# Softmax sums turned as one small transpose and spread through DRAM, the 256-key scores in split precision, another order of the query tiles, and the zero fills moved

## The reference, cut to what matters

```python
xn = _layernorm(x, axis=-1)                       # x: 8 batches x 512 tokens x 256
out = x + attention(xn) + moe(xn)                 # both in float32

# attention: 16 heads, latent keys/values of 64, rotary part of 64
norm_q  = rmsnorm(xn @ W_cq, q_scale);  norm_kv = rmsnorm(xn @ W_ckv, kv_scale)
scores  = einsum('bhqd,bhkd->bhqk', query, key) * scale      # 512 x 512 a head
attn    = softmax(where(causal, scores, -1e9), axis=-1)
attn_out = einsum('bhqk,bhkd->bhqd', attn, value) @ W_o

# moe: 32 experts, top 6, plus a shared expert
routed = einsum('tef,efd,te->td', silu(x@wg) * (x@wu), wd, combine)
```

## Time and profile before

| | |
|---|---|
| median of three runs | 1375.63 us |
| the profiled execution | 1372.54 us |
| its span | 1370.8 us |
| TensorE busy | 1268.6 us, 93% |
| VectorE busy | 898.7 us, 66% |
| ScalarE busy | 902.1 us, 66% |
| GpSimd busy | 631.3 us, 46% |
| stages, from the span's start | `project` from 30.2, `heads_first` from about 201, `experts` from 611, `heads_last` from about 960 us |

### The profile page before, as it was taken

The page is one execution under the profiler, slowest core; times in us unless marked ns, Lnnn a source line. Parts: engine busy times, 40 slices in busy tenths (PEclk is TensorE's granted clock), DMA queues, the critical chain, the costliest instruction groups (busy, mean ns, idle before and its releaser), DMA issues. The chain is left out here.

```text
span 1370.8 us, 25128 instructions
## 1 busy us (share of the span) xinstructions
PE 1268.6 (93%) x7640; PEld 999.6 (73%) x7641; DVE 898.7 (66%) x2823; ACT 902.1 (66%) x2462; POOL 631.3 (46%) x550
## 2 busy tenths in 40 slices
PE   4899859999999899979999999998899999999997
PEld 3566547778777678758788888887678777877775
DVE  3578778988888788823333333332787888788783
ACT  1455428777777587735566666665797788788783
POOL 1111108877776677730000000000888878878881
PEclk8899979999999999999999999999899999999999
DMA  9988663323236532239876666664555655655652
GB/s 347 362 288 283 258 234 117 111 98 115 97 110 231 175 105 97 90 110 338 320 247 188 188 181 199 186 186 148 108 84 86 103 107 89 128 86 97 104 70 47
DMA packets 150870, 223.32 MB, mean 163 GB/s; under 512 B 13846, under 2 KB 128214, under 8 KB 149462
## 3 DMA queue, kind: packets, MB, share of 16 engines
q1 hardware_dynamic: 102934, 157.72, 34.4%
q0 software_dynamic: 36864, 53.50, 19.0%
q10 hardware_dynamic: 10944, 10.49, 2.5%
HBM read 105.27 MB, written 116.39 MB: 162 GB/s over the span
## 5 line engine op out<-in xcount | busy, mean ns | idle before, releaser
L1580 POOL DMA_INDIRECT l_sums<-sorted_y,slot_no x192 | 308.1, 1605 | 59.3 <-issue 57.6
L1072 POOL DMA_INDIRECT sorted_x<-f_xn_row,slot_no x192 | 198.2, 1032 | 49.2 <-issue 44.5
L2184 DVE SCALAR_TENSOR_TENSOR act_f<-hidden,rows_in,ps 128x96 f32<-128x96 f32 x224 | 70.4, 314 | 228.5 <-ACT hidden L2147 228.4
L1257 ACT ACTIVATE f_prob<-f_prob,f_negmax 128x256 f32<-128x256 f32 (+3 forms) x256 | 142.7, 558 | 84.1 <-DVE f_negmax L1345 82.0
L2109 PE MATMUL ps<-wgu_sb,xt_e 128*128 x896 | 184.2, 328 | 0.4 <-issue 0.2
L1762 ACT ACTIVATE l_prob<-l_prob,l_negmax 128x256 f32<-128x256 f32 (+3 forms) x256 | 141.6, 554 | 62.1 <-DVE l_negmax L1862 60.7
L1587 POOL TENSOR_TENSOR l_k_lo<-l_kt,l_k_hi 128x512 fp32r<-128x512 f32 x4 | 5.1, 1273 | 368.7 <-ACT l_k_hi L1755 368.7
L1862 DVE CUSTOM_DVE_ANT_0 l_prob<-ps,mask_add 128x256 f32<-128x256 f32 (+3 forms) x256 | 119.9, 486 | 51.4 <-PE ps L66 37.6
L1345 DVE CUSTOM_DVE_ANT_0 f_prob<-ps,mask_add 128x256 f32<-128x256 f32 (+3 forms) x256 | 117.7, 482 | 45.5 <-PE ps L66 40.5
L2109 PEld LDWEIGHTS ps<-wgu_sb,xt_e 128*128 128x128 f32 x896 | 140.0, 190 | 3.2 <-issue 2.6
L2127 PE MATMUL ps<-wd_sb,at 96*128 x448 | 139.1, 392 | 1.1 <-issue 0.5
(11 more groups left out here) (212 smaller groups left out, 3168.9 us busy)
## 6 DMA issues: line engine op xcount, KB each, us to landing
sorted_x<-zeros SPq DMA_DIRECT2D x14, 2304.0 KB, 9.9
rows_in<-sorted_x SPq DMA_DIRECT2D x112, 288.0 KB, 3.2
sorted_y<-rows_out SPq DMA_DIRECT2D x112, 256.0 KB, 2.1
wgu_sb<-in_wgu SPq DMA_DIRECT2D x16, 384.0 KB, 5.7
x_in<-in_x SPq DMA_DIRECT2D x8, 512.0 KB, 10.5
xn_dram<-xn SPq DMA_DIRECT2D x8, 512.0 KB, 3.9
base_dram<-x_in SPq DMA_DIRECT2D x8, 512.0 KB, 2.9
nqt_dram<-nqt_out SPq DMA_DIRECT2D x8, 512.0 KB, 3.9
```

Of the source, the lines that this page charges most:

```text
L1072: pool.indirect_dma_start(sorted_x, bass.IndirectOffsetOnAxis(ap=slot_no[:, t, k:k + 1], axis=0), xn_row[buf][:], None).then_inc(scattered ...
L1257: act.activation(prob[:, i, qt, 0:w], prob[:, i, qt, 0:w], ACT.Exp, bias=negmax[:, i, qt:qt + 1], scale=-1.0, accum_out=rowsum[:, g // 2 % ...
L1580: pool.indirect_dma_start(sums[n % NSUM][:, t, :], None, sorted_y, bass.IndirectOffsetOnAxis(ap=slot_no[:, TT * GROUPS[n] + t, k:k + 1], a ...
```

## The change

1. The sums are turned before the reciprocal is taken: one transpose of `rowsum` (128 x 8) to 8 x 128, at the end of the even step, after `scores(3)`. VectorE takes the reciprocal of 8 partitions x 128 numbers from PSUM, after `maxima(3)` and ahead of `turned`.
2. SyncE stores the 8 x 128 inverses to `norms_dram`, waits for that, and loads them back, repeated over 64 partitions, with two transfers into `norms`. `spread_inverses`, `turn_norms` and `copy_norms` go from GpSimd, ScalarE and TensorE.
3. `FIRST_SPLIT` is 1: the 256-key scores are three float32r products; `q_hi` and `q_lo` are 384 wide.
4. `Q_ORDER` is `[0, 3, 2, 1]`: 128, 512, 384, 256 keys.
5. SyncE follows the same `pipeline(step)`; the stores of folded weights and the first loads of expert weights are cut up and spread over its steps.
6. The four early zero fills go from the first block to `project`: bodies 0 to 3 now have two fills each, ahead of the load of the next tokens.

```diff
-Q_ORDER = [1, 3, 2, 0]
-FIRST_SPLIT = 2
+Q_ORDER = [0, 3, 2, 1]
+FIRST_SPLIT = 1
...
-                sp.wait_ge(zeros_made, 1)
-                for i in range(EARLY):
-                    sp.dma_start(zero_part[i], zeros[:].unsqueeze(1).to_broadcast([P, zero_part.shape[2], ZCOLS]))\
-                        .then_inc(zeros_stored, 16)
...
-                if EARLY + i < ZFILLS:
-                    sp.dma_start(zero_part[EARLY + i], zeros[:].unsqueeze(1).to_broadcast([P, zero_part.shape[2], ZCOLS]))\
+                for n in ((2 * i, 2 * i + 1) if i < EARLY else (EARLY + i,)):
+                    sp.dma_start(zero_part[n], zeros[:].unsqueeze(1).to_broadcast([P, zero_part.shape[2], ZCOLS]))\
                         .then_inc(zeros_stored, 16)
...
+            def spread_inverses(b, p):
+                sp.wait_ge(rinv_ready, NP_ * b + p + 1)
+                sp.dma_start(norms_dram[p % 2], inverse[:, p % 2, :]).then_inc(norms_stored, 16)
+                sp.wait_ge(norms_stored, 16 * (NP_ * b + p + 1))
+                sp.wait_ge(lat_normed, NP_ * b + p)
+                for i in range(2):
+                    sp.dma_start(norms[i * KVR:(i + 1) * KVR, :].rearrange("r (t q) -> r t q", t=TT),
+                                 norms_dram[p % 2, i * TT:(i + 1) * TT, :].unsqueeze(0).to_broadcast([KVR, TT, P]))\
+                        .then_inc(norms_loaded, 16)
+            def keep(n):
+                k, at = n // (2 * QUART), n % QUART
+                part = slice(2 * at, 2 * at + 2)
+                if n // QUART % 2 == 0:
+                    sp.dma_start(wq_dram[k][:, part], wq_s[k][:, part].bitcast(F32)).then_inc(kept, 16)
+                else:
+                    sp.dma_start(wvo_dram[k][:, part], wvo_s[k][:, part].bitcast(F32)).then_inc(kept, 16)
+            def step(bt, g):
+                if g % 2 == 0 and bt.back(g, 2):
+                    spread_inverses(bt.back(g, 2)[0], bt.back(g, 2)[1] // 2)
...
+                if g % 2 == 1 and g < NH:
+                    if b > 0 and bt.next_pair(p):
+                        sp.wait_ge(q_ready, 2 * (NP_ * b + p + 2))
+                    if b in (1, 2):
+                        keep(NP_ * (b - 1) + p)
+                    if b == 3 and p == 0:
+                        sp.dma_start(rope_dram, rope_t[:]).then_inc(kept, 16)
+                    if b == 3 and 0 < p < 1 + (KC + 1) * weights.EARLY:
+                        weights.load_part(sp, (p - 1) // (KC + 1), (p - 1) % (KC + 1), wgu, wd)
...
 (TensorE)
-            def turn_norms(b, p):
+            def turn_sums(b, p):
                 pe.wait_ge(q_abs, min(NH * b + 2 * p + 6, NH * HB))
-                pe.wait_ge(spread_ready, NP_ * b + p + 1)
-                for t in range(TT):
-                    mm = pe.transpose(norms_ps[:, t * P:(t + 1) * P],
-                                      spread[:, p % 2, t].rearrange("p i n -> p (i n)"), ident[:])
-                mm.then_inc(norms_turned, 1)
+                pe.wait_ge(exp_done, unit(b, 2 * p + 2))
+                pe.transpose(sums_ps, rowsum[:, p % 2].rearrange("p i t -> p (i t)"), ident[:]).then_inc(sums_turned, 1)
...
                 if g < NH:
                     scores(bt.now, g, 3)
+                if par == 0 and bt.back(g, 2):
+                    b, h = bt.back(g, 2)
+                    turn_sums(b, h // 2)
...
 (VectorE)
             def inverses(b, p):
-                dve.wait_ge(exp_done, unit(b, 2 * p + 2))
-                dve.reciprocal(rinv[:, p % 2], rowsum[:, p % 2]).then_inc(rinv_ready, 1)
+                if NP_ * b + p > 1:
+                    dve.wait_ge(norms_stored, 16 * (NP_ * b + p - 1))
+                dve.wait_ge(sums_turned, NP_ * b + p + 1)
+                dve.reciprocal(inverse[:, p % 2, :], sums_ps).then_inc(rinv_ready, 1)
...
-                dve.wait_ge(norms_copied, NP_ * b + p + 1)
+                dve.wait_ge(norms_loaded, 32 * (NP_ * b + p + 1))
                 dve.tensor_tensor(lat[:, p % 2, :], o_ps, norms[:], ALU.mult).then_inc(lat_normed, 1)
...
                 if now:
                     maxima(bt.now, g, 3)
+                if par == 0 and bt.back(g, 2):
+                    b, h = bt.back(g, 2)
+                    inverses(b, h // 2)
                 if par == 0 and bt.back(g, 1):
                     turned(*bt.back(g, 1))
```

More of the change, by code:

```diff
@@ L423, in body @@
                 sp.dma_start(nkv_dram[i], nkv[:]).then_inc(nkv_stored, 16)
+            sp.wait_ge(zeros_made, 1)
             store_tokens(0)
@@ L1050, in _ @@
-            sp.wait_ge(kept, 16 * 5)
+            pipeline(step)(sp)
+            sp.wait_ge(kept, 16 * (4 * QUART + 1))
             for buf in range(ROWS):
@@ L1563, in _, with spread_inverses @@
-            for b in range(HB, B - 1):
-                during(b)
+            def spread_inverses(b, p):
+                sp.wait_ge(rinv_ready, NP_ * b + p + 1)
+                sp.dma_start(norms_dram[p % 2], inverse[:, p % 2, :]).then_inc(norms_stored, 16)
+                sp.wait_ge(norms_stored, 16 * (NP_ * b + p + 1))
+                sp.wait_ge(lat_normed, NP_ * b + p)
+                for i in range(2):
+                    sp.dma_start(norms[i * KVR:(i + 1) * KVR, :].rearrange("r (t q) -> r t q", t=TT),
+                                 norms_dram[p % 2, i * TT:(i + 1) * TT, :].unsqueeze(0).to_broadcast([KVR, TT, P]))\
+                        .then_inc(norms_loaded, 16)
```

182 lines of the change are left out of this document (77 added, 105 removed).

## The result

The changed kernel takes 1407.1 us (median of 4 runs, 1405.4 to 1410.1) against 1375.6 us beside it: 1.0228 times as long, with a 95% interval of 1.0209 to 1.0248. The profiled execution took 1408.0 us, with a span of 1406.3 against the 1370.8 of the earlier trace rows: 35.5 us more.

The account below looks back on a forecast made before the run. The prediction took TensorE to set the heads' pace, with VectorE only 1 us behind. Heads 26, stage ends 4, earlier start -3.7 and `project` 15 summed to 41 us more, 1416 on the median; 8-in-10 range 1386 to 1438.

Parts of the forecast that it names:

- The walk of the pair: Heads, plain pair: TensorE's wait for VectorE's copy, 0.7 us, replaces the removed transposes; 10.88 us, 0.30 more than 10.58.
- S: Heads: the time at which TensorE's last work of an even step is through; in the new order, the small transpose's end.
- The reciprocal: VectorE, even step: 8 partitions of 128 numbers take 0.95 us instead of 0.194, 0.76 more a pair.
- rival (a): Heads: reciprocal of 8 partitions costs 0.2 us, TensorE's saving comes through, pair 10.2 us; 1356 to 1370; 8 in 100.
- The pieces: Pairs with an output piece: queries wait for VectorE's residual, 0.3 us 28 times; first pieces in `heads_last` 0.3 more, 7 times.
- GpSimd's long wait: First stage of heads: the one long wait for GpSimd, 3.32 us, goes, since it no longer spreads the inverses.
- project and the start: `project`: second fill delays the tokens' load three times by 5.7 us, +15; engines start about 3.7 us earlier, -3.7.
- TensorE's cover: `project`: 2.9 us from normed tokens to their transposes, used up once; 3 x 5.7 - 2.9 = 14.2, VectorE late by 17.1.
- The tails: End of each heads stage: two DRAM hops of 5.5 us against 3.5 of values, so 2 us each, 4 in sum.
- The DRAM road: Inverses' store and load back: landed at S + 6.9, `latent_norm` at about S + 8.5, hidden in the loop with 1.6 us spare.
- rival (b): Last stage of heads: norms come late through DRAM, VectorE waits in every pair; 1464, or 1440 with 1 us; 12 in 100.
- The sum: Whole kernel: 26 + 4 - 3.7 + 15 = 41 us more, on the median 1416.

Follow-up runs that it names:

- e_copy_first: Changed kernel with VectorE's reciprocal behind its copy of the transposed probabilities instead of ahead of it: 1411.4 us, ratio 1.0249.
- e_load_first: Changed kernel with SyncE's load of the next tokens ahead of the two zero fills in each body of `project`: 1392.8 us, ratio 1.0119.
- the two fill experiments: Changed kernel with the tokens' load ahead of the fills: 1392.8 us; changed kernel with four fills in the first block, then one a body: 1398.5 us.

## Why the prediction was right, and where its sizes were off

**The walk of the pair** held in the last stage and in the first of two plain pairs in the first stage. It put `values` at S + 2.10, TensorE's waits at 0.7 us and the plain pair at 10.88; the trace has S + 2.02, 0.28 + 0.42 = 0.70 us, and 10.79. The step that is 0.08 us off is the copy (0.62 behind the reciprocal, where the row had 0.69). The same walk gives the other kernels that keep the reciprocal ahead of the copy, to 0.1 us: 10.73 against 10.68 with order and split back, 11.02 against 10.95 with the split back. It does not give e_copy_first: walked along TensorE alone that would be 10.2, and it is 10.68, since the delay runs on through VectorE's list. The prediction said that VectorE's 10.65 fits with 0.2 to spare, and that nothing queued behind the wait is needed sooner. In the last stage of the changed kernel VectorE does fit (10.43 of 10.79). But in the second of two plain pairs of the first stage it is busy 10.80 of 10.96 and the trace shows no wait of it of 0.1 us or more, and what stands behind the reciprocal is needed so soon that moving the copy ahead of it gained 0.11 us and not the 0.42 of the wait. The prediction names one of two paths that are nearly equally long.

**The reciprocal** was predicted at 0.95 from a row with 128 partitions and took 0.94; rival (a) fell with it. The prediction's estimate from the repeat count of 8 that the Trainium skill, VectorE: DVE Perf Modes, section First, the fixed hardware budget, gives was 1.07; the trace's 0.94 is below it.

**The pieces.** A second piece added 2.84 us to a plain pair and now adds 3.12 (predicted 0.3 more); a first one in `heads_last` 3.51 and now 4.09 (predicted 0.6 more). In `heads_first` the second piece costs only 0.1 more, 7 x 0.2 = 1.4 us less than forecast.

**GpSimd's long wait** was mis-sized. I took the 3.32 us of the earlier trace rows and no more. Before, the two pairs around it took 16.74 + 15.14 = 31.9 us, where their like elsewhere take 12.15 + 13.62; after, such pairs take 12.85 + 14.06. The stall was 31.9 - 25.8 = 6.1 us, since what it had delayed was paid for too, and none is left of it: 2.8 more than the term. With 0.08 us less in each of the last stage's 32 pairs (2.6; the first stage's +0.29 was as forecast) and the 1.4 of the pieces that is the 7 us by which the heads gave less, 19.0 instead of 26.

**project and the start.** Predicted +15 and -3.7. By its own first and last instructions `project` is 17.7 us longer and starts 4.1 us sooner; 1.5 us are won back before the first `values`, so that this comes 12.1 us later. Seen from the first small transpose, the hold-up is worth 16.3 us (e_load_first) and the start 3.9 (the difference of the two fill experiments). The load was issued at 60.33 and used at 75.34, 15.0 us against 16.2 predicted, and it held up VectorE three times, 5.3 to 6.4 us each. The 17.7 are near the 17.1 that the prediction had for VectorE, which it rounded down to 15 in favour of TensorE's cover.

**The tails**: 3.1 us for the last one against 2. The 1.4 for the first one's line hold `experts` too, which took 1.9 us more by itself, so that tail can't be read from them. **The DRAM road** in the loop was taken at nothing. VectorE waits for the norms 11.7 us in 9 places in the last stage, 4.5 of them in the tail; but only three pairs stand out, by 0.3 to 0.6 us each. That is rival (b) in small, 1 to 2 us.

**The sum** was 41 us, the spans differ by 35.5. The other 3 to 4 us of the miss (1416 against 1407.1) are the median over the profiled execution: it was 3.1 above it in the runs of before, and the changed kernel's is 0.9 below.

**Why the first stage's pair is 0.13 us longer** (10.92 against 10.79) can be read from the trace. From the small transpose on, TensorE's starts agree in the two stages to 0.02 us for 7.9 us. Then the first stage has this (GpSimd, VectorE, TensorE):

```profile
353.78 1.74 POOL L1116 TENSOR_TENSOR f_lat_lo<-f_lat,f_lat_hi 128x512 fp32r<-128x512 f32 x1 [3.67 <-ACT f_lat_hi L1291]
354.97 0.97 DVE L1351 TENSOR_TENSOR f_q_lo<-f_qt,f_q_hi 128x384 fp32r<-128x384 f32 x1
356.80 0.08 DVE L1359 DVE_READ_ACCUMULATOR2_ANT f_negmax<- 128x1 f32 x1
...
357.02 0.47 PE L64 MATMUL ps<-f_k_hi,f_q_hi 128*128 128x512 f32 x1
```

and the last this:

```profile
1130.30 0.08 DVE L1877 DVE_READ_ACCUMULATOR2_ANT l_negmax<- 128x1 f32 x1
...
1130.90 0.39 PE L64 MATMUL ps<-l_k_hi,l_q_hi 128*128 128x512 f32 x1
```

`f_q_lo` takes 0.97 us beside GpSimd's `f_lat_lo` where it takes 0.56 without, so the 256-key maxima behind it end at 356.88, and the 512-key score that needs their bank starts 0.14 us after that and as slowly as behind the other waits. In the last stage the maxima are through 0.52 us before it. In the 26 pairs where the two operations overlap, `f_q_lo` ends 0.41 to 0.43 us after `f_lat_lo` has ended. This is read from one trace; no run was made without `f_lat_lo`.

What remains open: why some kernels take 3 us more in `experts`, and how much of the last stage's differences is the road through DRAM, whose late norms fall on other pairs in each execution.

## What to carry to other kernels

Two engines that wait for each other within a period are one loop: walk it from start to start, over both, and expect that a delay moved behind one consumer comes out at the next if the engine has no gap behind it. Count the list of each engine too: a walk along one of them alone gave the time of the changed kernel and missed that of the swap. Put the cheap form of an operation ahead of the layout change (a reciprocal of 8 numbers a partition, then the transpose), not the dear one behind it. What a loop's next step needs goes into a queue ahead of bulk stores; and when tiles are reordered, look which maxima the next product into the same bank must wait for, and with how much cover.

## What the runs showed of the hardware

- VectorE's reciprocal follows the numbers on one partition and not the number of partitions: 0.19 us for 128 x 8, 0.94 for 8 x 128, 0.95 for 128 x 128.
- A 4 KB store to DRAM took from 1.22 us with idle DMA engines to 4.39 with busy ones (0.90), from its issue to the issue that waits for it.
- A load behind 2 fills in one queue took 15.0 us to be usable; issued 0.4 us ahead of them it made VectorE wait no longer, with the same bytes moving (medians to landing 10.8 and 5.5 us).
- Writing the 384-wide `q_lo` on VectorE takes 0.56 us alone. Where GpSimd's `f_lat_lo` runs beside it, in 26 of the first stage's 32 pairs, it takes mostly 0.97, and it ends 0.41 to 0.43 us after GpSimd's operation whenever it began. The maxima, which read the scores from PSUM, take 0.56 us for 384 keys beside the same operation, as elsewhere.
